# A PDE step and a mixture of experts on one core: the front rebuilt, the first expert in plain float32

## The reference, cut to what matters

```python
# x: (8, 128, 128). First a PDE step on every batch:
Af = A_grid[None] * f[:, None];  Bf = B_grid[None] * f[:, None]
gradv  = _grad(Af[:, 0], 1) + _grad(Af[:, 1], 2)
gradvv = _grad2(Bf[:, 0], 1) + _grad2(Bf[:, 1], 2) + _grad(_grad(Bf[:, 2], 2), 1) + _grad(_grad(Bf[:, 2], 1), 2)
x = maximum(f + (-gradv + 0.5 * gradvv) * dt[:, None, None], 0.0)
# then normalisation over features, over tokens, a style net, and 8 experts, 2 per token:
h = (x - mean) * rsqrt(var + 1e-5) * ln_g + ln_b          # over features
h = (h - h.mean(1)) * rsqrt(h.var(1) + 1e-8)              # over tokens
gamma, beta = small net of the batch's embedding;  gamma = softplus(gamma) + 1e-8
h = h * gamma + beta
probs = softmax(h @ router_w);  gates = top-2 of probs, divided by their sum
hid = relu(h @ exp_w1[e] + exp_b1[e])                     # 128 -> 512, every expert, every token
y = sum over e of gate[e] * (hid @ exp_w2[e] + exp_b2[e]) # 512 -> 128
return x + y
```

## Time and profile before

| | us |
|---|---|
| median of 3 runs | 136.35 (135.20 to 136.53) |
| the profiled execution | 136.27 |
| its span, first to last instruction | 134.4 |
| PE busy, 532 matmuls | 119.8 |
| DVE busy | 102.8 |
| ACT busy | 84.3 |
| mean granted PE clock, of full | 0.937 |

### The profile page before, as it was taken

How to read it: one execution, slowest core, us unless ns; L and a number is a source line. 1 busy time by engine, 2 the same in 40 slices (tenths; PEclk the granted TensorE clock), 3 DMA queues, 4 the chain that set the end, 5 groups by cost and what they waited for, 6 DMA issues and landing times.

```text
span 134.4 us, 1729 instructions
## 1 busy us (share of the span) xinstructions
PE 119.8 (89%) x532; PEld 93.5 (70%) x532; DVE 102.8 (76%) x214; ACT 84.3 (63%) x105; POOL 18.8 (14%) x29
## 2 busy tenths in 40 slices
PE   6652999679979999699999999999999999999980
PEld 2241797554668778488888888888888888888860
DVE  0589906899698993499699499499679959959872
ACT  3320129045479978837867888678776888678910
POOL 3198009860300000000000000000000000000030
PEclk9975557977999999999999999999999999999999
DMA  4999950000000002650040031004004004000004
GB/s 125 268 325 419 419 233 0 0 2 5 0 0 0 0 0 89 235 156 5 0 156 2 0 102 54 0 9 147 0 0 156 5 0 132 24 0 0 0 0 156
DMA packets 4310, 10.84 MB, mean 81 GB/s; under 512 B 648, under 2 KB 1608, under 8 KB 4304
## 3 DMA queue, kind: packets, MB, share of 16 engines
q1 hardware_dynamic: 3904, 10.39, 21.9%
q10 hardware_dynamic: 368, 0.38, 1.0%
q0 software_dynamic: 32, 0.00, 0.0%
HBM read 10.21 MB, written 0.56 MB: 80 GB/s over the span
## 4 chain that ended last, share of the span: by engine, by line
PE 74%; DVE 12%; DMA 8%; ACT 2%; issue 1%; ACTq 1%; DVEq 0%
PE yt L709 10%; PE yt L713 10%; PE yt L710 10%; PE zt L693 10%; PE zt L695 9%; PE zt L694 9%; DVE rows_lo L820 4%; DMA gt<-in_grids_exchanged_dram 4%; PE zt L623 3%; DMA gate_all<-gates_dram 3%; PE yt L609 1%; PE yt L616 1%; DMA gates_dram<-gateT 1%; PE zt L657 1%; PE zt L583 1%
## 5 line engine op out<-in xcount | busy, mean ns | idle before, releaser
L1046 DVE TENSOR_TENSOR hid_lo<-hid,hid_hi 128x1024 fp32r<-128x1024 f32 x29 | 35.4, 1223 | 12.4 <-ACT hid L527 9.5
L524 ACT ACTIVATE hid_hi<-zt,b1s 128x1024 fp32r<-128x1024 f32 x29 | 32.4, 1116 | 18.3 <-PE zt L695 18.3
L527 ACT ACTIVATE hid<-zt,b1s 128x1024 f32<-128x1024 f32 x29 | 32.1, 1108 | 0.0
L709 PE MATMUL yt<-hid_hi,ws 128*128 128x512 f32 (+1 forms) x64 | 25.1, 392 | 1.3 <-DVE yg L1083 1.3
L713 PE MATMUL yt<-hid_lo,ws 128*128 128x512 f32 (+1 forms) x64 | 24.8, 388 | 0.0
L710 PE MATMUL yt<-hid_hi,ws 128*128 128x512 f32 (+1 forms) x64 | 24.5, 383 | 0.0
L693 PE MATMUL zt<-h_hi,ws 128*128 128x512 f32 x60 | 23.9, 398 | 0.0
L694 PE MATMUL zt<-h_hi,ws 128*128 128x512 f32 x60 | 23.6, 393 | 0.0
L695 PE MATMUL zt<-h_lo,ws 128*128 128x512 f32 x60 | 23.5, 392 | 0.0
L709 PEld LDWEIGHTS yt<-hid_hi,ws 128*128 128x128 f32 x64 | 12.0, 188 | 4.2 <-ACT hid_hi L524 1.7
L401 POOL TENSOR_TENSOR acc<-acc,yg 128x512 f32<-128x512 f32 x1 | 1.3, 1272 | 93.5 <-DVE yg L1130 93.5
(11 more groups left out here) (157 smaller groups left out, 141.4 us busy)
## 6 DMA issues: line engine op xcount, KB each, us to landing
we<-in_exp_w_dram SPq DMA_DIRECT2D x8, 512.0 KB, 8.7
gate_all<-gates_dram SPq DMA_DIRECT2D x8, 512.0 KB, 3.7
f<-in_x_dram SPq DMA_DIRECT2D x2, 256.0 KB, 4.2
ft<-in_x_exchanged_dram SPq DMA_DIRECT2D x2, 256.0 KB, 5.3
out_dram<-acc SPq DMA_DIRECT2D x1, 256.0 KB, 2.1
out_dram<-acc SPq DMA_DIRECT2D x2, 128.0 KB, 2.0
first<-grid_and_difference_dram ACTq DMA_DIRECT2D x1, 128.0 KB, 3.5
gn<-in_grids_dram SPq DMA_DIRECT2D x1, 128.0 KB, 3.7
```

The source lines that it names most:

```text
L524: act.activation(hid_hi[:, c, :], zt[c % 2][:], ACT.Relu, bias=bias).then_inc(hi_ready, 1)
L527: act.activation(hid[:, c, :], zt[c % 2][:], ACT.Relu, bias=bias).then_inc(hid_ready, 1)
L709: pe.matmul(out_ps, w_hi, hid_hi[:, c, tok], start=(c == 0), stop=False)
L1046: v.tensor_tensor(hid_lo[:, c, :], hid[:, c, :], hid_hi[:, c, :].bitcast(F32), ALU.subtract).then_inc(lo_ready, 1)
```

## The change

The front and the first expert are written anew. The parts that the prediction speaks of:

1. Loads: `idi` moves from POOL's queue to SP's, `ft` from SP's to ACT's, `gt` from ACT's to SP's, `dtb` to POOL's; `mats` holds three matrices instead of two, and each expert's weights have a semaphore.
2. All row products are plain float32, in pieces of 256 columns; `rows_hi`, `rows_lo`, `diffs` and `neg_a0` are gone. DVE makes all products of half 0, POOL three of half 1. Each pair of batches has its own PSUM bank, so `advance` starts after the first pair.
3. ACT loads its function tables by name: log and exp first, the sqrt set after the softplus, ahead of `relu_step(0)`, which is now ACT's (both halves), the exp set ahead of `hidden0(0, 2)`.
4. POOL's `u_b1` of half 1 comes behind the softplus' last steps.
5. 8 zero matmuls at the start, 2 between two net layers, no others.
6. The first expert takes `h`, `we` and `hid` in plain float32: 16 matmuls of 512 columns (`layer1_0`, `layer2_0`), with no split of weights or of `hid`. The split of `h` and of expert 1's weights is DVE's.
7. The gates are not divided by the softmax's sum first; they are transposed by DVE in 32x32 blocks and stored by four DMAs. `router` stands between `low_part(1, 0)` and `low_part(1, 1)`, `gated(0)` and `add_up(0)` behind `low_part(1, 3)`.
8. Two y tiles in turn (`yt`, `aux`); the loops over experts are written out, biases are read where they lie.
9. In DVE's list `add_up(e - 1)` stands ahead of `low_part(e, 2)`, and `split_weights(e + 1)` behind it.

```diff
@@ loads of SP @@
             load(f[:, 0:BH, :], x[:, 0:BH, :], f_in[0])
+            load(idi[:], ids.partition_broadcast(NS), ids_in)
             load(gn[:], grids, gn_in)
-            load(ft[:, 0:BH, :], xT[:, 0:BH, :], ft_in[0])
             load(mats[:], const, mats_in)
+            load(gt[:], gridsT, gt_in)
+            load(f[:, BH:B, :], x[:, BH:B, :], f_in[1])
             load(pv[:], p128, p128_in)
...
+            for i in range(P // BLK):
+                stored = gates_dram.rearrange("(j u) (b i p) -> i (u b) j p", j=2, b=B, p=BLK)
+                sp.dma_start(stored[i], gateT[i * BLK:(i + 1) * BLK, :, :]).then_inc(gates_stored, 16)
@@ POOL @@
+            hb = batches(1)
+            pool.wait_ge(a0_ready, 2)
+            pool.wait_ge(gn_in, 16)
+            pool.tensor_tensor(u_b0[:, hb, :], f[:, hb, :], over_batches(gn[:, 1, :]), ALU.mult).then_inc(b0_ready[1], 1)
+            pool.wait_ge(ft_in[1], 16)
+            pool.wait_ge(gt_in, 16)
+            pool.tensor_tensor(u_a1[:, hb, :], ft[:, hb, :], over_batches(gt[:, 1, :]), ALU.mult).then_inc(a1_ready[1], 1)
+
+            pool.wait_ge(glog_ready, 1)
+            step(pool.tensor_tensor(gsum[:], gpos[:], glog[:], ALU.add))
+            step(pool.tensor_scalar(gamma[:], gsum[:], 1e-8, None, ALU.add))
...
+            pool.tensor_tensor(u_b1[:, hb, :], ft[:, hb, :], over_batches(gt[:, 0, :]), ALU.mult).then_inc(b1_ready[1], 1)
@@ ACT @@
+            act.preload_act_table_set("natural_log_exp_and_others")
...
+            def softplus():
+                act.wait_ge(net_ps, 5)
+                style = pv[:, STY_BG:STY_BG + 1]
+                act.activation(gabs[:], small[:, 0:B], ACT.Abs, bias=style).then_inc(gabs_ready, 1)
+                act.activation(gpos[:], small[:, 0:B], ACT.Relu, bias=style).then_inc(net_sb, 1)
...
+                act.activation(gexp[:], gabs[:], ACT.Exp, scale=-1.0).then_inc(gexp_ready, 1)
+                act.activation(beta[:], small[:, B:2 * B], ACT.Identity, bias=pv[:, STY_BB:STY_BB + 1]).then_inc(net_sb, 1)
...
+                act.activation(glog[:], gexp[:], ACT.Ln, bias=one[:, 0:1]).then_inc(glog_ready, 1)
...
+            net()
+            softplus()
+            act.preload_act_table_set("sqrt_and_others")
+            relu_step(0)
+            sd_features(0)
+            normalise(0)
+            relu_step(1)
+            sd_tokens(0)
+            transposed_step(0)
+            sd_features(1)
+            normalise(1)
+            conditioned(0)
+            transposed_step(1)
+            hidden0(0, 0)
+            hidden0(0, 1)
+            sd_tokens(1)
+            act.preload_act_table_set("exp_and_others")
+            hidden0(0, 2)
+            hidden0(0, 3)
@@ PE @@
+            keep_warm(WARM_START)
+            pe.wait_ge(first_in, 16)
+            step_cross(0)
+            pe.wait_ge(mats_in, 16)
+            rows_a(0)
+            rows_b(0)
...
+            net_layer(0, pw[0:NS, EMB_AT:EMB_AT + SE], onehot[:], SE)
+            keep_warm(WARM_GAP)
+            net_layer(1, pw[:, HW1_AT:HW1_AT + SH], se[:], SH)
+            columns_w(0)
...
+            net_layer(2, pv[:, HW2_AT:HW2_AT + SH], hyp1[:], SH)
+            columns_b(0)
+            net_layer(3, pv[:, SW1_AT:SW1_AT + SE], hyp2[:], SE)
+            step_cross(1)
+            pe.wait_ge(net_sb, 4)
+            pe.matmul(small[:, 0:B], pw[:, SW2_AT:SW2_AT + P], sty1[:], start=True, stop=True)
+            pe.matmul(small[:, B:2 * B], pw[:, SW2_AT + P:SW2_AT + 2 * P], sty1[:], start=True,
+                      stop=True).then_inc(net_ps, 1)
+            rows_a(1)
+            rows_b(1)
+            columns_w(1)
+            columns_b(1)
+            pe.wait_ge(xp_ready, BH)
+            norm_transposed(0)
+            step_transposed(0)
+            step_transposed(1)
+
+            wait_for_h(0)
...
+            layer1_0(0, 0)
+            layer1_0(0, 1)
+            pe.wait_ge(xp_ready, B)
+            norm_transposed(1)
+            layer1_0(0, 2)
+            pe.wait_ge(acc_ready, 2)
+            layer1_0(0, 3)
+            for c in range(C):
+                layer2_0(0, c)
+            wait_for_h(1)
+            logits()
+            for c in range(C):
+                layer1_0(1, c)
+            for c in range(C - 1):
+                layer2_0(1, c)
+            pe.wait_ge(h_hi_ready, 1)
+            pe.wait_ge(h_lo_ready, 1)
+            layer1(1, 0)
+            layer2_0(1, C - 1)
+            layer1(1, 1)
+            layer1(1, 2)
+            for e in range(1, E):
+                for c in range(C):
+                    if e == E - 1 and c >= C - 2:
+                        continue
+                    layer2(e, c)
+                    ahead = C * (e - 1) + c + LAG
+                    if ahead < C * (E - 1):
+                        layer1(1 + ahead // C, ahead % C)
+            last_layer2()
@@ DVE @@
+            product(u_a0, f, 1, gn[:, 0, :]).then_inc(a0_ready, 1)
+            advance(0)
             v.wait_ge(p128_in, 16)
+            squared = mark(v.tensor_scalar(gsq[:], ln_g, ln_g, None, ALU.mult))
+            feature_stats(0)
             cross_operand(1)
             normalise(0)
             advance(1)
             v.wait_ge(dve, squared)
+            moved = token_stats(0)
+            feature_stats(1)
+            scale_and_shift(0, moved)
             normalise(1)
             conditioned(0)
+            moved = token_stats(1)
+            scale_and_shift(1, moved)
             conditioned(1)
             input_parts()
+            split_weights(1)
             router_start()
...
+            for e in range(1, E - 1):
+                low_part(e, 0)
+                if e > 1:
+                    gated(e - 1)
+                else:
+                    router()
+                low_part(e, 1)
+                if e > 1:
+                    add_up(e - 1)
+                low_part(e, 2)
+                split_weights(e + 1)
+                low_part(e, 3)
+                if e == 1:
+                    gated(0)
+                    add_up(0)
```

More of the change, by code:

```diff
@@ L562, in _, with router_exponents @@
-            pair(0, first=True)
-            with act.Fori(1, E // 2 - 1) as i:
-                pair(i)
-            pair(E // 2 - 1, final=True)
+                    act.activation(hid_hi[:, c, half(n)], z_ps, ACT.Relu, bias=bias).then_inc(hi_ready, 1)
+                    act.activation(hid[:, c, half(n)], z_ps, ACT.Relu, bias=bias).then_inc(hid_ready, 1)
+            def router_exponents():
+                act.wait_ge(ld_ready, 1)
+                act.activation(ex[:], ld[:], ACT.Exp).then_inc(exp_ready, 1)
@@ L568, in _ @@
+            for e in range(1, E):
+                for c in range(C):
+                    if e == E - 1 and c == C - 1:
+                        last_hidden()
+                    else:
+                        hidden(e, c)
+                    if e == 1 and c == 0:
+                        router_exponents()
         @block.tensor
         def _(pe):
-            def net_layer(n, weights, acts, rows):
-                pe.matmul(small[0:rows, 0:B], weights, acts, start=True, stop=True).then_inc(net_ps, 1)
@@ L647, in _, with net_layer @@
-            step_columns_w(1)
-            step_columns_b(1)
-            def step_transposed(n):
-                if n == 0:
-                    pe.wait_ge(xs_ready, 1)
-                else:
-                    pe.wait_ge(xs_act_ready, 2)
-                for b in range(BH):
-                    last = pe.transpose(xsT[n][:, b * P:(b + 1) * P], xs[:, n * BH + b, :], ident)
+            def net_layer(n, weights, acts, rows):
+                if n > 0:
+                    pe.wait_ge(net_sb, n)
+                pe.matmul(small[0:rows, 0:B], weights, acts, start=True, stop=True).then_inc(net_ps, 1)
@@ new lines, in columns_b @@
+            def columns_b(n):
+                pe.wait_ge(b1_ready[n], 1)
+                for b in range(n * BH, (n + 1) * BH):
+                    last = pe.matmul(own(b), u_b1[:, b, :], half_diff2, start=False, stop=True, skip_group_check=True)
+                    if b % 2 == 1:
+                        last.then_inc(df_ready, 1)
+            def step_transposed(n):
+                pe.wait_ge(xs_ready, 2 * (n + 1))
+                pe.wait_ge(w_op_ready, n + 1)
+                for b in range(n * BH, (n + 1) * BH):
+                    last = pe.transpose(one_batch(zt[1], b), xs[:, b, :], ident)
@@ L681, in logits, with layer1_0 @@
+            def logits():
+                for b in range(B):
+                    last = pe.matmul(lg_ps[:, b * E:(b + 1) * E], one_batch(h, b), pv[:, RW_AT:RW_AT + E],
                                      start=True, stop=True)
                 last.then_inc(logits_ready, 1)
-            norm_transposed(0)
-            for n in range(HALVES):
-                step_transposed(n)
-            keep_warm(WARM_NORM)
-            norm_transposed(1)
-            def layer1_half(c, slot, n):
```

(9 more changed lines are left out.)

868 lines of the change are left out of this document (304 added, 564 removed).

## The result

| | before | after |
|---|---|---|
| median, us | 136.29 (135.20 to 136.53) | 146.77 (146.21 to 148.95) |
| ratio to before | | 1.088 (1.080 to 1.095) |
| profiled execution, span | 136.27, 134.4 | 146.21, 144.4 |
| PE busy | 119.8 | 121.3 |
| DVE busy | 102.8 | 91.3 |

The change makes the kernel slower, by 8.8% in the recorded ratio, which goes by the fast runs; the quotient of the two medians is 1.077, and the record doesn't show where that difference comes from. The sign was forecast, the size was not: 6.4 us more were forecast and 10.5 measured. The median of 146.77 is inside the range of 138.3 to 147.5, near its top; 8.8% on 136.35 would be 148.3, just outside.

The account below looks back on a forecast made before the run. PE was taken to bound the expert stage, any wait lengthening the run. Front to `layer1(1, 0)` 47.1 us plus 93.8 behind it, including 11.2 of split waits, gave span 140.9; with 1.87 outside, 142.8 us, range 138.3 to 147.5.

Parts of the forecast that it names:

- S: Start of `layer1(1, 0)`, the second expert's first layer, where the front ends; forecast at 47.1 us.
- The stage: Span from the start of `layer1(1, 0)` to the end; forecast 93.8 us, of which 11.2 are waits for splits.
- The late split: DVE's weight split behind `low_part(e, 2)`: PE 1.4 us late in each expert, 12.5 us per expert instead of 11.1.
- The first two turns: First two experts after S: weight split 2.9 us late for `layer1(2, 0)`, another 2.6 late for the next.
- late gates: Gates back from DRAM at S+14.9; DVE stands until then and stays full; next split 13.7 us after the last.
- The loads: Front: `mats` lands 5.4 us after issue, at 7.5, bounding the row products; `idi` and `dtb` moves have slack.
- The clock: PE's half clock: one front drop costing 1.7 us, columns taken at 3.0, 1.7 for a start at half clock before S.
- The second rival: PE's clock falls oftener, in front and experts: 3 to 6 us more, near 147; chance 0.22.
- ACT's order: Front: sqrt table load, 1.3 us, ahead of `relu_step(0)` delays `cross_operand(1)`; PE 3.3 us without work before `columns_w(1)`.
- h to S: PE work from `h` of half 0 to `layer1(1, 0)`: 15.25 us, plus 1.7 for a start at half clock.
- The rival of the other side: Weight split is in time before `layer1(e+1, 0)`: 11.2 us of waits absent, 131.6, 3.4% faster; chance 0.10.
- the front brings some 5 us: Front and dropped waits together save some 5 us, against 11 that the late splits cost.

Follow-up runs that it names:

- Two experiments of opposite direction: Changed kernel with the weight split moved back early in DVE's list: 138.89 us; kernel before with only add_up early and split late: 146.26 us.
- a third: Changed kernel with split_weights(e + 1) put between add_up(e - 1) and low_part(e, 2): 138.74 us, ratio 1.021.
- a_relu_first: Changed kernel with relu_step(0) ahead of softplus and sqrt table load, and POOL's u_b1 of half 1 ahead of its wait for the logarithm: 141.76 us, ratio 1.044.
- a_router_early: Changed kernel with router exponents on ACT ahead of the experts' loop and the router on DVE ahead of low_part(1, 0): 144.58 us, ratio 1.063.
- a_loads: Changed kernel with the loads in the order of before (gn ahead, ft on SP, gt on ACT): 142.52 us, ratio 1.054.
- a_fill: Changed kernel with 12 zero matmuls behind step_transposed(1), ahead of the first expert: 144.47 us, ratio 1.070.
- a_five: Changed kernel with split early, router early, relu_step(0) first, loads in the order of before, and 12 zero matmuls before the first expert: 126.25 us, ratio 0.936.
- b_split_late: Kernel before with only DVE's list altered for experts 1 to 6: add_up ahead of low_part(e, 2), split_weights(e + 1) behind it: 146.26 us, ratio 1.076.
- three orders mended: Changed kernel with the split early, the router early and relu_step(0) first: 131.64 us, ratio 0.967.
- a_five_e0_less: a_five with seven of eight plain float32 first-expert products for half 1 on 256 of 512 columns, output not the reference's: 124.71 us, ratio 0.923.

## Why the prediction was right and where it failed

**The sum, term by term.** The profiled span is 144.4 where I had 140.9, so 3.5 us are to be placed. S is 1.6 later than forecast: the row products start at 8.83 in place of 7.5 (1.3 later), from there to `h` PE is 0.6 quicker than I had it, and from `h` to S 0.9 slower. The stage is 1.85 longer: 0.7 in the first turn, 0.3 in the second, 0.7 in the four that follow, 0.2 behind them. Two terms failed, the loads and the clock; the splits' own delay was right in kind and a little small.

**The late split (right, mis-sized).** I had PE 1.4 us late in each expert and a cycle of 12.5; it was 12.67. Two experiments of opposite direction show the mechanism, a third that it is `low_part`'s wait. The 0.17 missing is in the handshakes: the split was done at 88.04 and PE started at 88.19, where I took 0.05, and the matmul behind a wait is 0.08 slower. Over the four experts 0.7 us.

**The first two turns.** `layer1(2, 0)` came at S+12.83 where I had 12.1, mostly because `layer1(1, 0)` itself began with matmuls 0.63 apart and the chunk 0 pass of ACT started at S+2.0 in place of 1.6. The next came 13.96 later (I had 13.7), but not for my reason. I had DVE full to the brim with late gates. In the profile DVE stands idle ahead of that `low_part` too, and what takes the time is a drop of the clock, six matmuls at 0.43. a_relu_first, which has no such drop, has 13.0 there, and a_router_early 12.67. So the late gates cost 0.3, not 1.2, and the clock the rest, 1.0. The whole stage: 95.65 against 93.8, in which the sum as I wrote it (89.7 and the tail of 3.96) makes 93.7.

**The loads (the step that failed).** I took `mats` as landing 5.4 after its issue, as before, and the other moves as free, "slack on both sides". With the new order it landed 6.7 after its issue and `gn` 5.6, and the order of before brings them back to 5.6 and 3.5. That is 1.3 us at the first row product, the largest single miss. a_loads shows what the order is worth to the end: 4.1 us. That this is as much as the forecast lacks is chance, since a_loads also loses a stretch at half clock that my sum had priced (the 1.7 in the front).

**The clock (the rival that came true in part).** I took 1.7 us for one drop in the front, 1.0 for the columns and 1.7 for the first expert. The profile has a stretch of 3.4 us at 9.8, one at 23.5, 6.8 us from 30.3 and 3.4 at 61. So one drop in the front was right, 6.8 us in place of 3.4 stood before the first expert, and the one in the experts I had priced at nothing: these two are the second step that failed. The second rival, to which I gave 0.22, said this, at 147. It is hardly an independent case, as I treated it: it hangs on the waits that I forecast. The Trainium skill (TensorE: Matmul & The Clock Gate, Part 1) has PE fall to half rate after idling. The runs agree in the direction: twelve fillers in a gap, or 2.7 us less of waiting, took stretches away. They also show nearly the same waits with and without a drop behind them (2.70 before the columns and 0.67 with 1.90 in the experts, in the changed kernel and in a_loads), so a drop can't be forecast from one wait's length.

**ACT's order (right).** Wait of PE 2.70, forecast 3.3, cause as told; the table load was followed by the relu 1.30 after its start, so the drain that the Trainium skill (ScalarE: Activation LUTs, "What ACT_TABLE_LOAD costs") adds is not to be seen here either. Mending the order brings 4.8.

**h to S.** 17.8 against 16.95: the clock again. a_fill, at full clock there, takes 15.2, which is my 15.25 for the work; the half clock cost 2.6 where I took 1.7.

**The rival of the other side** (the split in time) is excluded by the six waits. My sentence that the front brings some 5 us was too kind: S of 48.7 is, with one product still to come, 0.5 us ahead of where the kernel before stood (47.31 for its `layer1(1, 0)`, with 12 matmuls of expert 0, 2.8, still to come). With five orders mended, S is 40.13 in a_five, 9.1 us ahead by the same count, and the kernel 6.4% under the one before.

What stays open: how much each of the clock's stretches costs by itself (they come and go together with the waits), whether `ft` or `idi` held `gn` and `mats` up, and why b_split_late lost 10.8 in the medians where six times 1.66 makes 10.0 and the profiles have 9.7; the difference is inside the scatter of the runs.

## What to carry to other kernels

In an engine whose list is in order, an operation whose operands are ready belongs ahead of one that waits, above all where the busiest engine waits for the former; count its end against the moment it is asked for, before and after the move, because 1.2 us of room turned into 1.5 of delay here, and worse in the first turns, six waits in all. A large rewrite can be a gain and be hidden wholly by a few operations in the wrong place (8.8% slower as written, 3.3% faster with three orders mended, 6.4% with five), so time the parts of a large change apart. And a wait in front of TensorE can have a second price, half clock for the work behind it: of 1.1 us of later loads came 4.1.

## What the runs showed of the hardware that I had not expected

- A load of 128 KB (`gn`) landed 3.5 to 3.8 us after its issue with only `f` and `first` ahead of it (five kernels), and 5.6 to 6.1 with `ft`'s 256 KB and a small broadcast load in front as well (seven kernels). `mats` with 64 KB more landed after 5.5 to 5.7 in the old order (a_loads, a_five, a_five_e0_less), without them after 4.9 and 5.4 (b_split_late, before).
- The kernel before took nearly the same time with its clock full (0.994 to 1.0 over the span: 134.8 to 136.7 us, mean 135.3) and with 17 us at half (0.936 and 0.937: 135.2 to 136.8, mean 135.9), so PE's clock hardly sets the pace of its front. In the rebuilt front the 6.8 us at half clock before the first expert show in the time: a_fill, without them, is 2.1 shorter.
- A wait of PE costs 0.22 to 0.25 us more than its idle time in the profile reads, at 128x512 fp32r.
- In the kernel before, the one `rows_lo` of 5.7 us (7.90 to 13.63) ran beside four products of POOL in a row (8.14 to 13.07); the next `rows_lo` of the same shape, with POOL idle, took 0.68. A DVE product with one operand in PSUM took 0.69 beside POOL's (22.48). PE waited 2.69 us behind the long one, and the change has no `rows_lo`.
